# A two-branch feed-forward on one Trainium2 core: layer 1 multiplied once for the input and once for its twist, and the last state made in token order

## The reference, cut to what matters

```python
out = x                                     # layer-normed tokens, 256 wide
for _ in range(3):
    h = _gelu(out @ w1 + b1)                # 256 -> 256, "layer 1"
    h = _gelu(h @ w2 + b2)                  # 256 -> 128
    h = _gelu(h @ w3 + b3)                  # 128 -> 64
    tf = sigmoid(h @ w4 + b4)               # 64 -> 1
    combined = 0.7 * gf + 0.3 * tf          # gf: from the mean over the tokens
    coupling = 0.1 + adaptive_range * (combined - 0.5) * 2.0
    out = out + coupling * _twist(out)      # twist: [o_r, o_i, p_r, p_i] -> [p_r, -p_i, -o_r, o_i]
```

## Time and profile before

| | us |
|---|---|
| median of 3 runs | 1358.92 (1358.5 to 1360.76) |
| the profiled execution, whole | 1361.13 |
| its span in the trace | 1359.1 |
| f1, first normalised tile to its last instruction | 20.25 to 214.2 |
| f2, first normalised tile to the end | 1169.71 to 1359.1 |

### The profile page before, as it was taken

The page is one execution under the profiler, slowest core; times in us unless marked ns, Lnnn a source line. Parts: engine busy times, 40 slices in busy tenths (PEclk is TensorE's granted clock), DMA queues, the critical chain, the costliest instruction groups (busy, mean ns, idle before and its releaser), DMA issues. The chain is left out here.

```text
span 1359.1 us, 10889 instructions
## 1 busy us (share of the span) xinstructions
PE 1133.3 (83%) x2880; PEld 491.7 (36%) x2880; DVE 1149.4 (85%) x1628; ACT 737.0 (54%) x1267; POOL 871.9 (64%) x390
## 2 busy tenths in 40 slices
PE   3999985769778889878978987987896978799997
PEld 2344432223333334324324333433432423434443
DVE  4656676399999999999999999999999999746556
ACT  2554444757655756755656674665674433355442
POOL 0000000699989999998999999899999998000000
PEclk9999996798999999999999989999998988999998
DMA  6000000444535444354453544435435442000001
GB/s 201 0 1 1 0 0 1 140 135 146 180 102 185 132 149 155 124 185 134 146 179 113 174 146 139 151 124 186 154 127 184 155 156 78 0 0 0 32 31 62
DMA packets 46940, 146.47 MB, mean 108 GB/s; under 512 B 4448, under 2 KB 13280, under 8 KB 46880
## 3 DMA queue, kind: packets, MB, share of 16 engines
q1 hardware_dynamic: 46384, 144.96, 31.8%
q10 hardware_dynamic: 496, 0.82, 0.2%
HBM read 141.05 MB, written 4.72 MB: 107 GB/s over the span
## 5 line engine op out<-in xcount | busy, mean ns | idle before, releaser
L905 POOL TENSOR_TENSOR m_u<-m_dx,m_brow 128x1024 f32<-128x1024 f32 x256 | 596.7, 2355 | 1.0 <-DVE m_a_bank L988 0.9
L791 ACT ACTIVATE m_a_bank<-m_delta,m_negA 128x512 f32<-128x512 f32 x512 | 335.0, 683 | 171.6 <-DVE m_hc L1000 131.3
L1134 PE MATMUL m_y_bank<-m_hc,ident 128*128 128x512 f32 x640 | 333.1, 646 | 103.7 <-DVE m_hc L1000 103.7
L917 POOL TENSOR_TENSOR m_hc_pool<-m_hid,m_crow 128x1024 f32<-128x1024 f32 x96 | 226.0, 2354 | 28.5 <-DVE m_hid L988 28.1
L1134 PEld LDWEIGHTS m_y_bank<-m_hc,ident 128*128 128x128 f32 x640 | 120.1, 201 | 290.7 <-DVE m_hc L1000 170.5
L1000 DVE TENSOR_TENSOR m_hc<-m_a_bank,m_crow 128x512 f32<-128x512 f32 x320 | 202.5, 673 | 0.0
L926 POOL TENSOR_TENSOR m_dx<-m_delta,m_x 128x1024 f32<-128x1024 f32 x16 | 37.7, 2357 | 249.5 <-ACT m_delta L863 249.5
L988 DVE TENSOR_TENSOR_SCAN m_a_bank<-m_a_bank,m_carry,m_u 128x512 f32<-128x512 f32 x160 | 196.1, 1270 | 1.1 <-ACT m_a_bank L791 0.8
L988 DVE TENSOR_TENSOR_SCAN m_a_bank<-m_a_bank,m_u 128x512 f32<-128x512 f32 x160 | 186.6, 1212 | 7.1 <-POOL m_u L905 3.5
L1134 PE MATMUL m_y_bank<-m_hc_pool,ident 128*128 128x512 f32 x384 | 184.4, 603 | 5.6 <-POOL m_hc_pool L917 5.6
L333 PE MATMUL f_bank<-f_state,w 128*128 128x512 f32 x384 | 181.9, 603 | 0.0
(11 more groups left out here) (111 smaller groups left out, 1168.8 us busy)
## 6 DMA issues: line engine op xcount, KB each, us to landing
m_brow<-bc_rows SPq DMA_DIRECT2D x128, 512.0 KB, 4.8
m_crow<-bc_rows SPq DMA_DIRECT2D x128, 512.0 KB, 3.9
x_tok<-x_in SPq DMA_DIRECT2D x4, 1024.0 KB, 8.6
out<-x_tok SPq DMA_DIRECT2D x3, 1024.0 KB, 4.4
w<-w_in SPq DMA_DIRECT2D x1, 1024.0 KB, 11.4
out<-x_tok SPq DMA_DIRECT2D x2, 512.0 KB, 3.0
w<-w_in SPq DMA_DIRECT2D x1, 750.0 KB, 10.4
w<-w_in ACTq DMA_DIRECT2D x1, 512.0 KB, 5.9
```

The lines of the kernel that those rows point to most:

```text
L791: nc.scalar.activation(a_bank[K % 2][:, j, :], delta[:, i % 2, c, :], ACT.Exp, scale=negA[:, c, n:n + 1]).then_inc(S["a"], 1)
L905: nc.gpsimd.tensor_tensor(u[:, K % U_RING, :, :], dx[:, i % 2, 2 * q:2 * q + 2, :], brow[:, K // 2 % ROW_RING, K % 2, :].unsqueeze(1).to_b ...
L917: nc.gpsimd.tensor_tensor(hc_pool[:, before % POOL_RING, :, :], hid[:, before % POOL_RING, :, :], crow[:, K // 2 % ROW_RING, K % 2, :].uns ...
L1134: op = nc.tensor.matmul(y_bank[:, j, :], ident[:, :], source[:, before % ring, j, :], start=False, stop=K % PASS == PASS - 1)
```

## The change

`layer1` goes. Since a state is always z·p + twist(z)·q with one p and one q for each token, its product with w1 is A·p + B·q, where A = z @ w1 and B = twist(z) @ w1. The change makes A and B once for each batch and half (kinds "A" and "B" in the table `BESIDE`, L477 and L478; B is multiplied with the same weights and with their negative, `neg_w`), ACT copies both from PSUM to SBUF, and each cycle combines them:

- DVE's `update` makes the coupling c (L250), then a' = b·c + a over both channel blocks at once (L263, L265); gelu of layer 1 reads a' from SBUF. It runs for cycles 0 and 1 alone, no longer for the last cycle.
- POOL's `turn` makes b' = b - a·c (L370, L373) after cycle 0, and `keep` (L386) saves the couplings to a small tile `stack`.
- The host gives the channels in another order, so that the twist is a swap of the two blocks of 128 with a sign.
- The last state isn't kept: its three couplings per token are transposed to token order (kind "C", L484, eight transposes of 96 x 128), DVE makes from them the factors of each token (`coefficients`, 13 instructions of 128 x 8), and `finish` adds z·factor and the swapped z·factor to x_tok, six tiles of 128 tokens on DVE (L184, L186, L188) and two on POOL (L400 to L406). For this z_tok keeps all 32 tiles.
- The transposes "T" of z go by eight into a pair of banks, and ACT reads 128 x 1024 at a time. Each store of f2 is of 1 MB.

```diff
-    WORK += [(7, 4, "back", 1, 0), (8, 0, "back", 1, 1), (8, 1, "back", 1, 2), (8, 4, "back", 1, 3)]
...
-    WORK += [(TAIL, 0, "back", 2, t) for t in range(1, 4)] + [(TAIL, 1, "back", 3, t) for t in range(4)]
...
+    def step(b, c):
+        return b // 2 * 2 * CYCLES + 2 * c + b % 2
...
+    BESIDE = [
+        (HEAD, 0, "T", 0, 0, HEAD, 0), (HEAD, 0, "T", 0, 1, HEAD, 0),
+        (HEAD, 0, "A", 0, 0, HEAD, 0), (HEAD, 0, "A", 0, 1, 0, 1),
+        (0, 0, "B", 0, 0, 0, 2), (0, 1, "B", 0, 1, 0, 2), (0, 2, "g", 0, 0, 0, 3),
...
+        (6, 0, "C", 0, 0, None, None), (7, 0, "C", 1, 0, None, None), (11, 3, "C", 2, 0, None, None),
+        (TAIL, 1, "C", 3, 0, None, None),
+    ]
...
+    PAIR_OF = {use: 2 + n if n < 2 else n % 2 for n, use in enumerate(USES)}
...
             def update(s, h):
 
-                b = batch(s)
+                b, n = batch(s), coupled(s, h)
+                c = cpl[:, b % 2, half(h)]
                 dve.wait_ge(th_ready, s * HALVES + h + 1)
-                nc.vector.tensor_scalar(couple[:, c], th[:, c], slope[:, 0:1], base[:, b:b + 1], ALU.mult, ALU.add)\
-                    .then_inc(updated, 1)
-                dve.wait_ge(updated, before + 1)
-                nc.vector.tensor_tensor(turned[:, 0, c], couple[:, c], state[:, 1, cs], ALU.mult)\
-                    .then_inc(updated, 1)
-                nc.vector.tensor_tensor(turned[:, 1, c], couple[:, c], state[:, 0, cs], ALU.mult)\
-                    .then_inc(updated, 1)
-                dve.wait_ge(updated, before + 3)
-                nc.vector.tensor_tensor(state[:, 0, cs], state[:, 0, cs], turned[:, 0, c], ALU.add)\
-                    .then_inc(updated, 1)
-                nc.vector.tensor_tensor(state[:, 1, cs], state[:, 1, cs], turned[:, 1, c], ALU.subtract)\
-                    .then_inc(updated, 1)
...
-            def add_back(b, t):
-                tiles = x_tok[:, b * BT + 2 * t:b * BT + 2 * t + 2, :]
-                nc.vector.scalar_tensor_tensor(tiles, bank[bank_of(*use)][:, :].rearrange("p (a d) -> p a d", a=2),
-                                               0.5, tiles, ALU.mult, ALU.add).then_inc(back_added, 1)
+                nc.vector.tensor_scalar(c, c, slope[:, 0:1], base[:, b:b + 1], ALU.mult, ALU.add).then_inc(coupling, 1)
+                dve.wait_ge(coupling, n)
+                if cycle(s) == 0:
+                    wait_read(dve, ("B", b, h))
...
+                    to, other = a1[:, b % 2, :, half(h)], a[:, b % AB_RING, :, half(h)]
+                else:
+                    dve.wait_ge(b_ready, turned(step(b, 0), h))
+                    dve.wait_ge(a_ready, coupled(step(b, 0), h))
...
+                    to, other = a[:, b % AB_RING, :, half(h)], a1[:, b % 2, :, half(h)]
+                nc.vector.tensor_tensor(to, b_[:, b % AB_RING, :, half(h)], over_m(c), ALU.mult).then_inc(scaled, 1)
+                dve.wait_ge(scaled, n)
+                nc.vector.tensor_tensor(to, to, other, ALU.add).then_inc(a_ready, 1)
...
+            def coefficients(b):
...
+                for j in range(2):
+                    nc.vector.tensor_copy(split(j), src[:, :, :, 32 * j])
+                nc.vector.tensor_scalar(split(2), src[:, :, :, 64], slope[:, 0:1], base[:, b:b + 1],
...
+                nc.vector.tensor_tensor(at(3), at(0), at(1), ALU.mult)
+                nc.vector.tensor_tensor(at(4), at(0), at(1), ALU.add).then_inc(coef_part, 1)
...
+                nc.vector.tensor_scalar(at(7), at(6), -0.5, 0.5, ALU.mult, ALU.add)
+                nc.vector.tensor_scalar(at(8), at(5), 0.5, None, ALU.mult)
+                nc.vector.tensor_scalar(at(9), at(5), -0.5, None, ALU.mult).then_inc(coef_ready, 1)
+                dve.wait_ge(coef_ready, b + 1)
...
+            def finish(b):
+
+                coefficients(b)
+                for t in range(DVE_TILES):
+                    op = add_back(b, t, True)
+                op.then_inc(first_added, 1)
+                dve.wait_ge(first_added, b + 1)
+                for t in range(DVE_TILES):
+                    add_back(b, t, False)
...
+                    normalise(2)
                     coupling_base(1)
...
+                if s in (6, 7):
+                    finish(s - 6)
                 if s in (9, 10) and measure_next:
                     measure(s - 9)
...
+            finish(2)
+            finish(3)
             if measure_next:
+                measure(2)
                 measure(3)
+
...
+            def turn(s, h):
...
+                nc.gpsimd.tensor_tensor(part[:, :, :], a[:, b % AB_RING, :, half(h)], over_m(c), ALU.mult).then_inc(part_ready, 1)
+                pool.wait_ge(part_ready, turned(s, h))
+                pool.wait_ge(scaled, coupled(s, h))
+                nc.gpsimd.tensor_tensor(b_[:, b % AB_RING, :, half(h)], b_[:, b % AB_RING, :, half(h)], part[:, :, :], ALU.subtract)\
+                    .then_inc(b_ready, 1)
...
+            def keep(s, h):
...
+                nc.gpsimd.tensor_copy(stack[n:n + 32, b % 2, half(h)], cpl[n:n + 32, b % 2, half(h)])\
+                    .then_inc(kept, 1)
+                pool.wait_ge(kept, coupled(s, h))
...
+            def finish(b):
...
+                pool.wait_ge(coef_ready, b + 1)
+                pool.wait_ge(b_ready, turned(step(b, 0), 1))
...
+                nc.gpsimd.tensor_tensor(straight, zs, by(7, DIM), ALU.mult).then_inc(finish_part, 1)
+                nc.gpsimd.tensor_tensor(across[:, :, :P], zs[:, :, P:], by(8, P), ALU.mult)
+                nc.gpsimd.tensor_tensor(across[:, :, P:], zs[:, :, :P], by(9, P), ALU.mult).then_inc(finish_part, 1)
+                pool.wait_ge(finish_part, 3 * b + 1)
+                nc.gpsimd.tensor_tensor(xs, xs, straight, ALU.add).then_inc(finish_part, 1)
+                pool.wait_ge(finish_part, 3 * b + 3)
+                nc.gpsimd.tensor_tensor(xs, xs, across, ALU.add).then_inc(added_pool, 1)
...
+            for s in range(STEPS):
+                if s in (6, 7):
+                    finish(s - 6)
+                if cycle(s) < CYCLES - 1:
+                    for h in range(HALVES):
+                        if cycle(s) == 0:
+                            turn(s, h)
+                        keep(s, h)
+            finish(2)
+            finish(3)
...
-                    last = nc.tensor.matmul(bank[h * 2 + m][:, :], w(w256, W256, "w1", k)[:, m * P:(m + 1) * P],
-                                            state[:, k, cs], start=k == 0, stop=k == KD - 1)
-                last.then_inc(l1_done, 1)
...
+                if kind == "T":
+                    pe.wait_ge(z_ready, b * BT + (n + 1) * HB)
...
+                        for i in range(HB):
+                            last = nc.tensor.transpose(out[:, k, i * P:(i + 1) * P],
+                                                       z_tok[:, b * BT + n * HB + i, k * P:(k + 1) * P], ident[:, :])
+                elif kind in ("A", "B"):
+                    wait_read(pe, ("T", b, n))
+                    if kind == "B":
+                        pe.wait_ge(constants, 1)
+                    for m in range(KD):
+                        ms = slice(m * P, (m + 1) * P)
+                        if kind == "A":
+                            first, second = w(w256, W256, "w1", 0)[:, ms], w(w256, W256, "w1", 1)[:, ms]
+                        else:
+                            first, second = neg_w[:, ms], w(w256, W256, "w1", 0)[:, ms]
+                        nc.tensor.matmul(out[:, m, :], first, z[:, b % 2, 0, half(n)], start=True, stop=False)
+                        last = nc.tensor.matmul(out[:, m, :], second, z[:, b % 2, 1, half(n)], start=False, stop=True)
+                elif kind == "C":
...
+                    for t in range(BT):
+                        last = nc.tensor.transpose(out[:, t // HB, t % HB * P:t % HB * P + STACK],
+                                                   stack[:, b % 2, t * P:(t + 1) * P], ident[0:STACK, 0:STACK])
...
+            beside(HEAD, 0)
             for s in range(STEPS):
-                layer1(s, 0, 0)
+                beside(s, 0)
                 if s > 0:
                     layer3(s - 1)
-                side(s, 0)
-                layer1(s, 0, 1)
+                beside(s, 1)
+                layer2(s, 0)
                 if s > 0:
                     layer4(s - 1)
-                side(s, 1)
-                layer1(s, 1, 0)
-                side(s, 2)
-                layer1(s, 1, 1)
-                side(s, 3)
-                layer2(s, 0)
-                side(s, 4)
+                beside(s, 2)
                 layer2(s, 1)
+                beside(s, 3)
             layer3(STEPS - 1)
-            side(TAIL, 0)
             layer4(STEPS - 1)
-            side(TAIL, 1)
+            beside(TAIL, 1)
```

More of the change, by code:

```diff
@@ L282, in _ @@
             coupling_base(0)
-            def adds(s, places):
-                for place in places:
-                    for kind, b, t in due(s, place):
-                        if kind == "back":
```

(39 more changed lines are left out.)

383 lines of the change are left out of this document (213 added, 170 removed), and 10 rows, old and new, of the table BESIDE.

## The result

| | us, median | ratio to before, 95% interval |
|---|---|---|
| before | 1358.9 | |
| after | 1435.3 (1434.5 to 1435.7) | 1.056 [1.054, 1.058] |
| forecast | 1385 (range 1334 to 1402) | |

A forecast was written before the change was run, and what follows sets the result against it. The prediction took PE's work to set the length of a step, with DVE's update hidden. -28.6 undisturbed, +50 turns and +5 clock give +26.4 on the profiled 1361.13, 1387.5; less 2.2 for the median, 1385, range 1334 to 1402.

The forecast's parts named there:

- turns: DVE and POOL on SBUF wait for each other's whole instructions: 25 us a call, +50; chance 0.58 (1385).
- (c): Stage 1: update(0) later by up to 6.3, so PE waits for `normalise(2)` in step 2: +0.8 to +4.7.
- nothing disturbed, with the clock: Both calls, every engine at its own pace: -28.6, plus +5 for falls of PE's clock.
- (a): update(6) and update(7): DVE waits for POOL's four products, +2.35 to +6.3 an update.
- Stage 1: First normalised tile to step 6: PE's work and waits 105 us in f2, +15.1; +13.6 in f1.
- the upper bound of 61.6: Both `ffn` calls: DVE and POOL take strict turns, whole instructions at a time; 30.8 a call.
- (b): `finish`: DVE's 4.5 and POOL's 5.1 no longer overlap, +4.5 in `finish(1)`, +9 for the two at the end.
- POOL's yielding: DVE keeps its pace in `ffn` and only POOL is late: 1350 to 1370, chance 0.12.
- the case without contention: DVE and POOL don't disturb each other in `ffn`: 1335, range 1328 to 1346, chance 0.24.
- Clock, stage 2: Steps 8 to 11: pauses drop PE to half clock; one fall a call, +5, bounds 0 and 20.
- Stage 2 undisturbed: Steps 6 to 11, bound by the loop tanh, update, gelu: 51.3 in f2, -30.6; -29.8 in f1.
- Stage 3 undisturbed: The end, two finishes and last store: 19.8 in f2, +2.2; 21.1 in f1, +0.9.

The follow-up runs named there:

- all_thin: both_thin with POOL's five instructions of `finish` also cut to 2 elements of a row (work left out): 1345.6 us, ratio 0.990.
- turn_thin: The changed kernel with POOL's two instructions of `turn` cut to 4 elements a partition (b' not made): 1394.4 us, ratio 1.025.
- both_thin: both_first with POOL's two products of `turn` also cut to 4 elements a partition (b' not made): 1366.4 us, ratio 1.005.
- both_first: sum_first with `normalise(2)` and `normalise(3)` also put ahead of update(0) and update(1) on DVE: 1394.3 us, ratio 1.026.
- the fill: The changed kernel with idle PE products, results unused, put into PE's pauses in steps 8 to 11: 1430.8 us, ratio 1.052.
- sum_first: The changed kernel with `sum_up(2)` and `sum_up(3)` put ahead of the updates of steps 2 and 3 on DVE: 1406.3 us, ratio 1.034.

## Why the prediction was wrong

The runs give a ledger, each entry a difference of two medians: before 1358.9; the change with turns and queue taken away 1345.6 (-13.3; this is `all_thin`, which leaves POOL's work out and keeps POOL's small copies); turns in `finish` +20.7; turns in `turn` +27.9; DVE's queue in stage 1 +41.0; sum 1435.3. Against it stood -28.6 + 5, and 50 for all turns.

The order of taking away matters for the last two entries, and the prediction's own terms want the other order: it had the wait for `normalise(2)` among the turns, as (c). Take the turns away first, with the queue as it is (after against `turn_thin`), and they are worth 40.9 + 20.7 = 61.6; the queue that is left (`turn_thin` against `both_thin`) is worth 28.0, the sums' waits.

| | forecast | measured |
|---|---|---|
| nothing disturbed, with the clock | -28.6 + 5 = -23.6 | -13.3 |
| turns, (a) to (c) | +50 | +61.6 |
| other waits of PE in stage 1 | 0 | +28.0 |

- **Stage 1, failed: the list of PE's waits.** The sum of PE's work was right: 105 forecast, 105.1 and 105.3 in `both_first`, with PE busy in 100.8 (98.4 + 1.9 forecast) and idle in 4.3 (1.4 + 3.4). But "PE stops for ACT's reads of shared banks (...), 3.4 as I followed it" followed ACT alone. I didn't follow `total`: `sum_up(2)` and `sum_up(3)` were priced at nothing. They cost 28 to 29 by the medians, 25.0 in stage 1 of the traces. It isn't that an update became longer, as the two updates ahead of the sums take 6.6 us each and have no turn; the change moved PE's reading of the sums further forward than the sums. The last sentence of the prediction, "if stage 1 has waits on PE that I haven't followed", is the case that came.
- **Turns, right in kind, too small in size.** "They take strict turns, whole instructions at a time": so it is, to the tenth of a microsecond. But I took 50 of the upper bound of 61.6, "because DVE won't lose every time", and the runs give the bound. No row stood behind that discount. That the sum agrees to the tenth is luck, since the parts don't: (a) 27.9 for both calls, bound 25.2. The updates take the 12.4 of the bound; 1.9 more a call are the factors of `finish(1)`, whose small L281 waits for POOL's last subtraction (1.86 for 0.37). (b) 20.7, bound 27: one finish costs 3.5 to 3.6, not 4.5, and in f1 most of that of stage 2 is hidden by a fall of the clock. (c) 13.0, bound 9.4: PE waits 6.60 for `normalise(2)`, since update(0) is longer by 6.3 and the normalising, one input, takes turns too, and behind the wait PE is at half clock. POOL's yielding and the case without contention are out.
- **The skill's rule.** The trace agrees with "SBUF — State Buffer", Who interferes with whom, of the Trainium skill: the two-input L265 takes 3.25 beside POOL's reads, 1.22 beside its writes. The same section lists `tensor_scalar` among the instructions that can block, too, when it runs in a two-port mode; I had used only its sentence on two inputs. L250's 2.57 and the normalising's 4.75 instead of 2.67 agree with that as well. That they run in such a mode is likely but not shown: L250 takes 0.54 for 512 elements and L278, of the same form, 0.28 for 8, so 504 elements add 0.26, where a two-input instruction adds 0.53 for 512 (0.69 to 1.22).
- **Clock, stage 2.** +5 forecast, 2.0 to 4.5 by the fill. **Clock, stage 1, failed:** not in the sum; 8.0 in f1, behind the waits. A wait of PE costs itself and then the slow records behind it.
- **Stage 2 undisturbed, mis-sized.** 51.3 forecast in f2, 56.9 in `all_thin`; 52.1 and 60.0 in f1. In f1: first tanh 12.9 for 12.0; `finish(1)` 7.6 for 6.4 (the add-backs L186 and L188 come every 0.26, not 0.2, and L184 takes 0.41, not 0.35); the four updates 25.8 for 24.4 (in six of their eight pairs of L263 and L265 a small copy of `keep` stands beside one of the two, 1.51 for 1.22); the wait for the tanh of step 8 4.7 for 2.6; the way from update(9) to the last gelu 5.8 for 3.3. The last two hold a layer 2 at half clock each (3.78 for 1.98). In f2 the clock had not fallen ahead of step 11, and the stage is 3 us shorter.
- **Stage 3 undisturbed, nearly right.** 19.8 forecast, 20.6; in f1 21.1 and 22.3. (Its terms add up to 14.8, not 15.0.) With turns 27.7, as in "the tail of f2 20 or 28".

The miss is 50.3: 28.0 of waits that weren't followed, 11.6 of turns, 10.3 of what was under-sized with nothing disturbed, and rounding. The range took in every price of the turns, and no case had a wait in stage 1 beyond them; but without the sums' waits (`sum_first`, 1406.3) the time would still lie 4 above it, with the turns at their bound and the stages under-sized.

## What to carry to other kernels

When an instruction of one engine becomes longer, or another engine's reading of a result is moved forward, list everything queued in front of that result and ask who waits for it, small things first: here two sums of 2 columns in each call, read by products of 128 x 1, cost 25 to 29 us, half clock behind the waits included. Work given to POOL isn't free while DVE works between tiles of SBUF as here (with an input from PSUM DVE kept its pace); count both engines' times as one sum wherever POOL reads, and put the work on the faster of the two (1.22 against 2.35 us for 128 x 1024). An engine that is 90% busy isn't thereby the bound: take work off it and see whether the idle time stays filled.
